# A fused decoder layer on one core: the low part of the gated product is subtracted on GpSimd instead of VectorE

## The reference

```python
x = x + rwkv(layernorm(x), Wk, Wv, Wr, Wo, ...)       # mix, k/v/r products, a scan over time, layer norm, Wo
x = x + wkv(xw, xu, layernorm(x), ctx_2048)           # a second scan over time, with a given v
...
g = einsum('th,ih->ti', xf, gate_w) * gate_s          # xf = layernorm(x), INTER = 1408
u = einsum('th,ih->ti', xf, up_w) * up_s
hdn = silu(g) * u
out = einsum('ti,hi->th', hdn, down_w) * down_s
x = x + out
```

## Time and profile before

| | |
|---|---|
| median of 3 runs | 667.77 us (666.24 to 667.82) |
| the profiled execution's own time: span | 664.8 us |
| TensorE busy | 555.3 us (84%) |
| VectorE busy | 549.1 us (83%) |
| ScalarE busy | 350.0 us (53%) |
| GpSimd busy | 24.1 us (4%), 39 instructions |
| line 686, hl on VectorE | 88 instructions, 35.8 us |

### The profile page before, as it was taken

How to read it: one execution, slowest core, us unless ns; L and a number is a source line. 1 busy time by engine, 2 the same in 40 slices (tenths; PEclk the granted TensorE clock), 3 DMA queues, 4 the chain that set the end, 5 groups by cost and what they waited for, 6 DMA issues and landing times.

```text
span 664.8 us, 8239 instructions
## 1 busy us (share of the span) xinstructions
PE 555.3 (84%) x2658; PEld 390.3 (59%) x2658; DVE 549.1 (83%) x1048; ACT 350.0 (53%) x572; POOL 24.1 (4%) x39
## 2 busy tenths in 40 slices
PE   3987582169999997789998997697998998799996
PEld 2433331067454766778453757687454757679995
DVE  6999998958999679977999859997899869996343
ACT  4546303326675428755765617764856516864231
POOL 1000000001000000001000000001000000000000
PEclk9998596559998998798999999699998998799999
DMA  8999000011010000011001000002002000000000
GB/s 313 372 373 380 1 0 0 0 33 33 0 64 1 1 16 17 0 45 52 0 2 61 0 0 32 0 10 86 0 0 64 0 0 32 0 0 33 1 33 34
DMA packets 11887, 34.73 MB, mean 52 GB/s; under 512 B 912, under 2 KB 912, under 8 KB 11664
## 3 DMA queue, kind: packets, MB, share of 16 engines
q1 hardware_dynamic: 11856, 34.37, 14.2%
HBM read 30.18 MB, written 12.85 MB: 65 GB/s over the span
## 4 chain that ended last, share of the span: by engine, by line
issue 68%; DVE 14%; PE 12%; POOL 2%; ACT 2%; DMA 1%; POOLq 0%; DVEq 0%; SPq 0%
PE gu L464 7%; PE dacc L387 4%; POOL t_rstd L342 2%; DVE t_otile L862 2%; DVE t_stats L643 1%; PE bank L362 1%; DVE t_num_st L734 1%; DVE t_num_st L800 1%; DVE t_pmax L713 1%; DVE t_slot L669 1%; DVE t_slot L670 1%; DMA t_xres<-in_x 1%; DVE t_gap L716 0%; DVE t_slot L745 0%; DVE t_otile L888 0%
## 5 line engine op out<-in xcount | busy, mean ns | idle before, releaser
L464 PE MATMUL gu<-t_z4h,t_gate 128*128 128x256 f32 x352 | 96.9, 308 | 28.7 <-DVE t_h L844 27.0
L464 PE MATMUL gu<-t_z4l,t_up 128*128 128x256 f32 x352 | 91.9, 293 | 0.0
L464 PEld LDWEIGHTS gu<-t_z4h,t_gate 128*128 128x128 f32 x352 | 70.1, 199 | 37.0 <-DVE t_h L844 30.7
L464 PE MATMUL gu<-t_z4h,t_up 128*128 128x256 f32 x352 | 91.7, 293 | 0.0
L464 PE MATMUL gu<-t_z4l,t_gate 128*128 128x256 f32 x352 | 90.4, 290 | 0.0
L600 ACT ACTIVATE t_silu<-gu,t_fsc 128x256 f32<-128x256 f32 x88 | 41.4, 476 | 87.6 <-PE gu L464 87.3
L387 PE MATMUL dacc<-t_down,t_hh 128*128 128x512 f32 x176 | 73.8, 419 | 2.0 <-DVE t_hl L686 1.7
L486 ACT ACT_TABLE_LOAD x57 | 73.1, 1283 | 1.7 <-PEq L926 0.7
L373 PE MATMUL bank<-t_z,t_wr 128*128 128x512 f32 x128 | 62.9, 642 | 13.0 <-DVE t_gap L736 11.4
L464 PEld LDWEIGHTS gu<-t_z4l,t_gate 128*128 128x128 f32 x352 | 70.2, 200 | 3.3 <-issue 2.2
L464 PEld LDWEIGHTS gu<-t_z4l,t_up 128*128 128x128 f32 x352 | 71.8, 204 | 0.0
(11 more groups left out here) (113 smaller groups left out, 977.4 us busy)
## 6 DMA issues: line engine op xcount, KB each, us to landing
t_xres<-in_x SPq DMA_DIRECT2D x8, 512.0 KB, 3.5
t_mixv<-in_ctx_t SPq DMA_DIRECT2D x4, 1024.0 KB, 5.5
out<-t_otile SPq DMA_DIRECT2D x16, 256.0 KB, 2.0
gate_words<-in_gate_t SPq DMA_DIRECT2D x1, 2816.0 KB, 17.8
up_words<-in_up_t SPq DMA_DIRECT2D x1, 2816.0 KB, 25.1
t_gate<-gate_words SPq DMA_DIRECT2D x1, 2816.0 KB, 15.5
down_words<-in_down_t SPq DMA_DIRECT2D x1, 2816.0 KB, 22.6
t_up<-up_words SPq DMA_DIRECT2D x1, 2816.0 KB, 21.2
```

The lines of the kernel that those rows point to most:

```text
L464: last = pe.matmul(gu[u % 2][:, side, :], as_read(w[:, k, i * P:(i + 1) * P], exact), as_read(part[:, k, hf * HALF:(hf + 1) * HALF], exact ...
```

## The change

The step `rest` is taken out of VectorE's list and put into GpSimd's, at the same place of BODY. It is the same subtraction with the same wait (hh_done) and the same signal (hl_done). In GpSimd's list it stands among the powers of the layer norms. VectorE keeps `prod`, which still waits for hl_done of three units before, now a signal from another engine. Nothing else differs.

```diff
@@ in the GpSimd program, step()
                     pool.tensor_tensor(rstd[:, half(k)], veps[:, half(k)], mhalf[:, half(k)], ALU.pow).then_inc(rstd_done, 1)
+                if s.startswith("rest"):
+                    u = int(s[4:])
+
+                    need(pool, hh_done, f, u + 1)
+                    pool.tensor_tensor(hl[:, u % 3, :], h[:, u % 3, :], hh[:, u % 3, :].bitcast(F32),
+                                       ALU.subtract).then_inc(hl_done, 1)
@@ in the VectorE program
-            def rest_h(u, f):
-
-                need(dve, hh_done, f, u + 1)
-                dve.tensor_tensor(hl[:, u % 3, :], h[:, u % 3, :], hh[:, u % 3, :].bitcast(F32),
-                                  ALU.subtract).then_inc(hl_done, 1)
-
@@ VectorE, step()
-                elif s.startswith("rest"):
-                    rest_h(int(s[4:]), f)
```

## The result

The change makes the kernel slower by 0.8%: 673.13 us, median of 4 runs (671.54 to 673.86), against 667.46 for the kernel before (4 runs); the ratio is 1.0083, interval 1.0067 to 1.0100. The forecast was 669.0, no change. The time lies in its range (658.0 to 674.5), but as a slower kernel, which had the smallest of its three chances (0.29, against 0.37 for faster and 0.34 for the same).

What follows compares the result with a forecast made beforehand. VectorE was taken to bound two stretches of a pass, TensorE the rest. Per pass -2.7 us saved and +3.1 us port price gave +0.4, three passes +1.2: 667.8 + 1.2 = 669.0 us, range 658.0 to 674.5.

Steps and rivals of the forecast that it cites:

- two stretches named as VectorE's: 317 to 371.5 and 402 to 437 us of a pass, said to move only as VectorE moves.
- The saving: Subtractions leaving VectorE: seven count, 2.3 us, plus 0.2 for a pair and 0.2 for powers; 2.7 us per pass.
- marginal price of 0.33 us: What one subtraction takes of VectorE's back-to-back work, less than its duration of 418 ns.
- The hold: GpSimd's reads share an SBUF port and delay VectorE's next two-input operation: 0.44 us each, 3.1 us per pass.
- The count of holds: Seven per pass: high4, high12, high14 to high18, where VectorE runs operations with two SBUF inputs and another follows.
- deciding price (0.48): Price in us per meeting, at seven per pass, from which a pass loses 0.67 us and the kernel reads as slower.
- signs named: Pass about 153.0 us; forecast wrong if it shrinks over 2 us or two-input rows grow over 0.5 at seven places.
- (a): Rival: VectorE is never held, GpSimd takes the port only when free; saves 8.1 us, 659.7 us; chance 0.28.
- (b): Rival: GpSimd keeps the port its whole 0.87 us at seven places, VectorE pays in full; 676.8 us; chance 0.26.
- (c): Rival: more removed subtractions count than seven; all 22 without port price save 21.8 us, 646; chance 0.06.
- (d): Rival: GpSimd's queue order delays a layer-norm power; needs a subtraction over 2 us; chance 0.03.
- The tail: Feed-forward steps after the last pass, TensorE's part; 0.5 us of slack at the last t_hl, so change 0.

Runs made afterwards that it cites:

- e1_write_only: Changed kernel, but GpSimd subtracts one column of 256 per unit and writes the other 255 by memset, reading nothing: 660.53 us, ratio 0.9902 to the kernel before.
- e9_best: Changed kernel with units 2, 4, 7, 12, 13, 15, 16 back on VectorE and GpSimd's 14, 17, 18 begun later: 664.27 us, ratio 0.9947 to before.
- e4_split: Changed kernel with the ten contended units (2, 4, 7, 12 to 18) back on VectorE, other twelve on GpSimd: 667.53 us, ratio 0.9997 to before.
- e3: Changed kernel, but GpSimd subtracts only one column of 256 per unit, the rest not computed: 661.28 us, ratio 0.9922 to the kernel before.

## Why the prediction was off

**The bounds held.** The two stretches named as VectorE's are the two that moved, and the part between them did not (23.29 and 23.31 us), although the power of stat3 there starts 0.9 us earlier.

**The saving was 2.7 us per pass by the sum; it is about 1.6.** The kernels without holds show it: e1_write_only's three passes are 1.7, 1.6 (the low clock's 1.1 left out) and 1.4 us shorter than before's. In parts: 0.32 in the attention stage, 1.0 in the second recurrence (44.44 to about 43.4), 0.16 between the powers of stat4_1 and stat1_0 (3.36 to 3.20), where the first of them fell from 0.79 to 0.69 us. The marginal price of 0.33 us was right where it was paid in full (unit 3). The count was too high. The subtraction at 365.65 (unit 4's) was taken as part of unbroken VectorE work; with it gone VectorE waits 1.31 us for TensorE at 371.86, where before it waited 0.31, so that one was free. And in the second recurrence seven removed bring 1.0 us and not 5 x 0.33 + 0.2 = 1.85; taking 11, 14, 17 and 18 away there (e9_best) brings only 0.16. A stretch that is 97% busy is VectorE's on the whole, but its chain changes hands several times (the wait for ScalarE in the earlier trace rows is one such place), and there a saving can be lost: in e1_write_only VectorE comes to the t_slot operation of 430.24 early and waits 0.88 us for ScalarE, where the kernel before has no wait.

**GpSimd's duration** was put at 0.65 us, from 0.49 to 0.87. It is 0.73 alone, within the bounds, and up to 1.29 with its own waiting. The queue delays no power: the closest, stat3's, follows its subtraction (389.66 to 390.39) by 0.6 us.

**The hold was the right mechanism.** Its price was put at 0.44 us net; a row shows 0.54. What the time pays per hold is less: after against e1_write_only 3.0 us for seven in the second recurrence, 0.43 each, 0.81 for two in the attention stage and nothing for unit 7's; in all 3.8 us per pass, against 3.1 in the sum. The read time behind it was taken as 0.50 and measured 0.54. The estimate from the Trainium skill, GPSIMD Engine Reference, section 3, with its 4497 ns for 2048 columns, was 0.56: with the hold (0.54), not with the instruction (0.73), the trace agrees.

**The count of holds was the step that failed**: seven per pass, and there are ten. The step high13 was listed as free, since the operation after it reads PSUM; but that subtraction starts when the third refine operation still has to start, and holds it (412.09 and 412.20 above). The two at t_nmr were never looked for: the text asked who reads hl after rest2 and did not ask what VectorE does while rest2 runs. It also looked only among long operations; an operation of two columns that costs 0.16 us is held for the same 0.5. The deciding price (0.48) was worked out for seven; with ten holds and a saving of 1.6 the kernel is the slower from (1.6 + 0.67) / 10 = 0.23 us per hold on. One kind of meeting stayed unseen until e4_split: VectorE's own subtraction has two inputs in SBUF and is held as well.

**The sum** was -2.7 + 3.1 = +0.4 per pass. It is -1.6 + 3.8 = +2.2, 6.7 us in three passes with the low clock's stretch left out; both terms were off towards the same side. The difference of the medians is 5.7. That 673.1 still lies in the range is in part luck: the upper end, 674.5, stood for seven holds at 0.70 us each, and no hold is longer than 0.55; more holds than counted and a smaller saving filled the room. Of the signs named, the rows at the seven places grew by 0.41 to 0.54 us, by over 0.5 at four of them, and the pass grew by 2.2 us (low clock left out) and not by 0.4. The 3.0 us set around the span are not all a cost around it: in the changed kernel's runs the time is 1.8 to 1.9 us above the span, so the profiled execution of before took, by estimate, 666.6 us and lay a good microsecond under the median that the forecast starts from.

**The rivals.** (a), never held, is what e3 and e1 make: 660.5 to 661.3, where it said 659.7. (b) had the right verdict with a wrong reason: the hold is not GpSimd's whole instruction, but 0.54 of 0.73 us with 256 columns, 0.27 of 0.46 with 128. The Trainium skill, SBUF — State Buffer, section Who interferes with whom, calls the shared ports an exclusive lock and says of VectorE's 2-port modes that the first to issue has them for the whole instruction; carried over to two-input work, as the prediction did, this does not hold here. That the issue order decides who waits, the same section's other point, the rows of 410 to 412 show. (c) and (d) did not occur.

**The tail** was given nothing. It is 61.44 us against 60.77. Of these 0.7 us, 0.4 lie ahead of TensorE's last product, 55.33 us behind the last power against 54.95; in e3_no_rest, without holds and with a shorter way from t_hh to t_hl, it is 54.87. The other 0.3 lie behind it, in the last additions and the store, a part that takes 5.6 to 7.5 us over the profiled runs. The 0.4 were not taken apart further.

## What to carry to other kernels

Moving elementwise work from VectorE to GpSimd saves only what VectorE's chain gives back (here 1.6 us per pass of the 22 x 0.33 = 7.3 that left the engine), and costs VectorE 2.1 ns per column wherever GpSimd's two-input operation meets one of VectorE with two inputs in SBUF. Count the meetings step by step, short operations behind a layer norm's power and the moved operation's own siblings on VectorE included, and move only the pieces that meet PSUM reads or idle time; that version is 0.5% faster here where the wholesale one is 0.8% slower. For a kernel tuned to this point compare stage lengths between fixed instructions as well as the total: here most of them repeat to 0.01 us from pass to pass while the total moves by 1 to 2 us, and one that does not repeat points to its own cause, such as the wait ahead of t_xf.

## What was not expected of the hardware

- A GpSimd operation with one SBUF input (copy of 255 columns, 0.39 us alone) stretches to 1.38 us beside VectorE's two-input work and holds VectorE by 0.08 to 0.20; with two inputs it holds it by up to 0.55. Writes alone (memset, 0.31 us) hold nothing.
- A VectorE operation of 2 columns with two SBUF inputs is held as long as one of 512: 0.16 to 0.68 us.
- The granted clock of a short stretch (0.84 or 1.00 at 296 to 304 us) differs between two nearly equal programs, and between the passes of one, and is worth 1.1 to 1.2 us each time.
